# A routed feed-forward kernel: token rows scattered as two planes of 16-bit halves, transposed by the DMA that loads them

## The chip, the cores and the metric

One core of a Trainium2 chip runs the whole program. The metric is device time in microseconds from launch to end, the median of three runs. Every time below is in microseconds (us) unless it says nanoseconds (ns).

## The reference

4096 tokens of 128 features go through three blocks, all in float32: half a feed-forward block with experts, an attention block, and the expert block once more.

```python
x = x + 0.5 * ffn(layernorm(x))
x = x + attn(layernorm(x))
x = x + 0.5 * ffn(layernorm(x))

def ffn(x):
    t = rmsnorm(x) * norm_scale
    vals, idx = top_k(t @ gate_w.T + gate_b, 4)      # 4 of 32 experts
    w = softmax(vals)
    combine[token, idx] = w
    h = swiglu(einsum('th,efh->tef', t, w1) + b1)     # 128 -> 2*128
    out = einsum('tef,ehf->th', h * combine, w2) + combine @ b2
    return x + out
```

Only the four chosen experts of a token count, so the kernel computes those alone. The attention block is linear in the tokens (no softmax over scores) and is not touched by the change.

## The kernel before, in words

**Two chunks, four phases.** The tokens are 32 tiles of 128, in two chunks of 16 tiles (c = 0, 1). An expert block is run twice (f = 0, 1), so there are four phases, ph = 2f + c. In `route` each phase normalises its tiles into `U`, turns them on TensorE, computes the gate, takes the top four, and works out for each of the 64 pairs (tile, choice) the row of a table in device memory to which each token goes.

**Scatter, experts, gather.** GpSimd (`scatter`, L519) issues 64 indirect DMAs a phase. Each writes 128 token rows of 512 bytes from `U` to the table `xs[c]`, sorted by expert, each expert's part padded to a multiple of 128 rows. The table has 96 tiles of 128 rows. `experts` takes it in groups of four tiles (GT = 4), 24 groups a chunk (NG), 48 a block (NGF). SyncE loads a group as 256 KB into `xrow` (L356) and stores its result `yrow` to `ys[c]` (L361). GpSimd (`gather`, L544) then fetches the rows back with 64 indirect DMAs a phase, and VectorE adds them with their weights to `X`.

**The step of the experts.** It is a software pipeline over the groups. In step k TensorE turns the four tiles of `xrow` of group k (`turn_rows`) and those of `hid` of group k-3 (`turn_hid`), forms the first product of group k-1 (four matrix products with 256 columns, `first_product`, L1311) and the second product of group k-4 (`second_product`, L1320). ScalarE copies the second product of group k-5 to `yrow` (L626), computes the gated function of group k-2 (L631), copies the turned `hid` of group k-3 to `hidT` (L634) and the turned rows of group k to `xT`, adding 1.0 (L639). VectorE clips the two halves of the first product (L1005, L1010) and multiplies them (L1018), and in some steps adds a gathered tile to `X` (L981). `xrow`, `xT`, `hid`, `hidT` and `yrow` have two buffers each. In PSUM the turned rows have two banks, the two first products two each, the turned `hid` one (`HT`) and the second product one (`YP`).

**The seam.** Group 24 is the first of chunk 1, and its rows are there only when all 64 DMAs of scatter(1) have landed. `seam` on TensorE and ScalarE writes out by hand the order around it: the work left over of chunk 0 stands interleaved with the start of chunk 1.

**What orders GpSimd.** Its order is fixed: scatter 0, scatter 1, gather 0, gather 1, scatter 2, scatter 3, gather 2, gather 3. Single DMAs also wait for the progress of the experts (`keep_to_experts`, L464: DMA i of a phase waits for a semaphore of a group number worked out from 36·i and an offset). A gather starts only when all 24 groups of its chunk are stored. Scatter 0 runs before the experts of block 0 start, scatter 1 and gather 0 beside them, gather 1 and scatter 2 beside attention and routing, scatter 3 and gather 2 beside the experts of block 1, and gather 3 alone at the end.

## Time and profile before

| | before |
|---|---|
| median of 3 runs | 724.93 us (724.14 to 725.18) |
| span of the profiled execution | 722.9 us |
| mean granted TensorE clock | 0.843 |
| TensorE busy | 531.0 us, 73% |
| weight loads | 443.8 us, 61% |
| VectorE busy | 436.2 us, 60% |
| ScalarE busy | 347.2 us, 48% |
| GpSimd busy | 506.2 us, 70% |
| moved by DMA | 108.28 MB, 150 GB/s over the span |

The median of the runs lies 2.0 us above the span of the profiled execution; the page gives the span, from the first instruction to the last. A busy share is an average over the whole program. The experts of block 0 lie at about 115 to 290 us, those of block 1 at about 460 to 633 us, attention and routing between them, and the last gather after them. GpSimd's 70% leave out about 0.3 us between two indirect DMAs, in which it is neither waiting for anybody nor free.

### The profile page before, as it was taken

How to read it: one execution, taken by the hardware profiler on the slowest of the kernel's cores; microseconds unless marked ns; L12 is line 12 of the kernel's file. 1: busy time of each engine (PE TensorE's matmuls, PEld its weight loads, DVE VectorE, ACT ScalarE, POOL GpSimd, SP SyncE). 2: the span in 40 equal slices, each digit the busy share in tenths (PEclk: the TensorE clock that was granted, in tenths of full speed). 3: DMA queues.
4: the chain of work that ended last, by engine and by line, in shares of the span. 5: the costliest groups of instructions: out<-in, count | busy, mean ns of one | idle time of the engine just before them, and what ended most of it. 6: DMA issues, size and time to landing. Idle time of an engine off the chain costs nothing. (4 is left out here: it accounts for less than half of the span.)

```text
span 722.9 us, 12843 instructions
## 1 busy us (share of the span) xinstructions
PE 531.0 (73%) x3252; PEld 443.8 (61%) x3253; DVE 436.2 (60%) x1243; ACT 347.2 (48%) x752; POOL 506.2 (70%) x551
## 2 busy tenths in 40 slices
PE   6258879999899999385607854999999999933000
PEld 3154366999899998253504553699998999833000
DVE  6889233555547778378993868255564767845222
ACT  4444413666556666495606644366665666610000
POOL 3677777777527777777677777777752777767765
PEclk9556999999999999797557955999999999977555
DMA  7997115566546664222111111456655666524222
GB/s 271 392 375 289 52 54 153 197 194 200 175 147 197 199 210 154 81 54 53 48 52 54 51 52 55 138 182 208 203 168 177 201 198 206 160 78 128 66 62 58
DMA packets 56493, 108.28 MB, mean 150 GB/s; under 512 B 12576, under 2 KB 19968, under 8 KB 56320
## 3 DMA queue, kind: packets, MB, share of 16 engines
q1 hardware_dynamic: 40064, 74.13, 30.7%
q0 software_dynamic: 16384, 33.59, 16.1%
q8 instruction: 23, 0.38, 0.2%
q14 instruction: 22, 0.18, 0.1%
...
## 5 line engine op out<-in xcount | busy, mean ns | idle before, releaser
L564 POOL DMA_INDIRECT YG<-ys,row x256 | 245.0, 957 | 116.9 <-issue 75.4
L539 POOL DMA_INDIRECT xs<-U,row x256 | 250.7, 979 | 81.9 <-issue 74.6
L1311 PE MATMUL PS<-W,xT 128*128 x768 | 182.2, 380 | 0.2
L1311 PEld LDWEIGHTS PS<-W,xT 128*128 128x128 f32 x768 | 138.4, 190 | 16.1 <-issue 1.2
L1005 DVE TENSOR_SCALAR glulin<-PS 128x512 f32<-128x512 f32 x96 | 66.3, 691 | 127.8 <-PE PS L1320 84.3
L626 ACT ACTIVATE yrow<-PS 128x512 f32<-128x512 f32 x96 | 57.3, 597 | 103.3 <-PE PS L1320 103.3
L1320 PEld LDWEIGHTS PS<-W,hidT 128*128 128x128 f32 x768 | 100.7, 193 | 7.8 <-issue 3.4
L1320 PE MATMUL PS<-W,hidT 128*128 x768 | 102.8, 277 | 1.6 <-issue 1.2
L1018 DVE SCALAR_TENSOR_TENSOR hid<-glulin,swish 128x512 f32<-128x512 f32 x96 | 66.6, 694 | 16.0 <-ACT swish L631 10.5
L631 ACT ACTIVATE swish<-glulin 128x512 f32<-128x512 f32 x96 | 60.4, 629 | 30.5 <-DVE glulin L1005 26.7
L639 ACT ACTIVATE xT<-PS 128x512 f32<-128x512 f32 x96 | 56.3, 589 | 38.8 <-PE PS L1214 38.7
L1010 DVE TENSOR_SCALAR glulin<-PS 128x512 f32<-128x512 f32 x96 | 65.3, 680 | 0.0
L1214 PE MATMUL PS<-ident,xrow 128*128 128x128 f32 x384 | 58.5, 275 | 3.9 <-DMA xrow<-xs 3.8
L1214 PE MATMUL PS<-ident,hid 128*128 128x128 f32 x384 | 58.1, 274 | 1.9 <-ACT hidT L634 1.9
L634 ACT ACTIVATE hidT<-PS 128x512 f32<-128x512 f32 x96 | 55.6, 579 | 0.9 <-PE PS L1214 0.9
L1214 PEld LDWEIGHTS PS<-ident,xrow 128*128 128x128 f32 x384 | 45.4, 142 | 7.3 <-DMA xrow<-xs 6.5
L1214 PEld LDWEIGHTS PS<-ident,hid 128*128 128x128 f32 x384 | 45.2, 141 | 2.3 <-DVE hid L1018 2.3
L1063 DVE SCALAR_TENSOR_TENSOR PS<-YG,wtop,X 128x128 f32<-128x128 f32 x40 | 12.4, 353 | 50.5 <-issue 44.5
L981 DVE SCALAR_TENSOR_TENSOR X<-YG,wtop,X (+1 forms) x96 | 32.8, 341 | 3.9 <-DMA YG<-ys,row 3.9
L1214 PE MATMUL PS<-ident,U 128*128 128x128 f32 x64 | 14.5, 386 | 24.7 <-ACT U L595 24.7
L1231 PEld LDWEIGHTS PS<-gw,xT 128*128 128x128 f32 x128 | 25.8, 296 | 6.0 <-issue 3.6
L583 ACT ACTIVATE vq<-vq 128x32 f32<-128x32 f32 x6 | 1.4, 229 | 58.2 <-DVE vq L808 58.2
...
## 6 DMA issues: line engine op xcount, KB each, us to landing
xrow<-xs SPq DMA_DIRECT2D x96, 256.0 KB
ys<-yrow SPq DMA_DIRECT2D x96, 256.0 KB
...
xs<-U,row POOLq DMA_INDIRECT x256
YG<-ys,row POOLq DMA_INDIRECT x256, 2.5
out<-X SPq DMA_DIRECT2D x7, 256.0 KB, 2.6
X<-in_x SPq DMA_DIRECT2D x4, 256.0 KB, 3.6
```

Source lines behind the costliest of these rows:

```text
L539: pool.indirect_dma_start(out=xs[c], out_offset=bass.IndirectOffsetOnAxis(ap=row[:, i:i + 1], axis=0), in_=U[:, (c * CT + t) * H:(c * CT + ...
L564: pool.indirect_dma_start(out=YG[:, t * TOPK + k, :], out_offset=None, in_=ys[c], in_offset=bass.IndirectOffsetOnAxis(ap=row[:, i:i + 1], ...
L626: a.activation(yrow[:, r, :], bank, ACT.Copy).then_inc(yrow_ready, 1)
L631: a.activation(swish[:, r, :], glu[:, r, :], ACT.Gelu_apprx_sigmoid).then_inc(swish_ready, 1)
L634: a.activation(hidT[:, r, :], HT, ACT.Copy).then_inc(hidT_ready, 1)
L639: a.activation(xT[:, r, :], TP[r], ACT.Copy, bias=1.0).then_inc(xT_ready, 1)
L1005: v.tensor_scalar(glu[:, s, :].rearrange("p (q f) -> p q f", q=GT), h1[:, 0], LIMIT, None, ALU.min).then_inc(glu_ready, 1)
L1010: v.tensor_scalar(lin[:, s, :].rearrange("p (q f) -> p q f", q=GT), h1[:, 1], -LIMIT, LIMIT, ALU.max, ALU.min).then_inc(lin_ready, 1)
L1018: v.scalar_tensor_tensor(hid[:, s, :], lin[:, s, :], 1.0, swish[:, s, :], ALU.add, ALU.mult)\
L1214: last = te.transpose(dst[:, q * P:(q + 1) * P], src[:, q * H:(q + 1) * H], ident[:])
L1311: last = te.matmul(h1, xT[:, r, q * P:(q + 1) * P], W[:, bass.ds(es[q], 2 * H)], start=True, stop=True)
L1320: last = te.matmul(bank[:, q * H:(q + 1) * H], hidT[:, r, q * P:(q + 1) * P], W[:, bass.ds(es[q] + 2 * H, H)], start=True, stop=True)
```

## The change

The normalised rows are no longer scattered as float32. In `route`, after the copies to `xT`, ScalarE adds 1.0 to four tiles of `U` at a time (into `hid`, which is free there) and then copies them to `planes`, where a token has 128 low halves of 16 bits and behind them 128 high halves, 512 bytes as before. These rows are scattered. The DMA that loads a group is a transposing DMA over 16-bit elements: it reads 512 rows of 256 halves and writes `xP` with 128 partitions of two planes of 512 halves. TensorE no longer turns rows; ScalarE's `join_rows` puts low and high halves together into `xT` (1024 elements of 16 bits a partition). The two PSUM banks that become free go to the turned `hid` and the second product, so that both have two. `U` shrinks to one chunk, and a few buffers are laid over others to make room for `planes`.

The seam is written in another order on TensorE, ScalarE and SyncE: chunk 0 is finished before chunk 1 starts. The offset of the gathers in `keep_to_experts` goes from 2750 to 2380.

```diff
-        U = sb("U", [P, NTILE * H])
+        U = sb("U", [P, CT * H])
+        planes = sb("planes", [P, NTILE * 2 * H], U16)
-        xrow = sb("xrow", [P, 2, GW])
+        xP = sb("xP", [P, 2, 2 * GW], U16)
-        HT = PS[:, 6, :]
-        YP = PS[:, 7, :]
+        HT = [PS[:, 0, :], PS[:, 6, :]]
+        YP = [PS[:, 7, :], PS[:, 1, :]]
-        xs_v = [a.rearrange("(g p q) h -> g p (q h)", p=P, q=GT) for a in xs]
+        xs_v = [a.bitcast(U16).rearrange("(g r) n -> g r n", r=GW) for a in xs]
...
                 def load(c, k, r):
-                    wait_count(sp, turned, k + (t0 - 4 if c == 0 and isinstance(k, int) and k < 2 else t0 - 1))
-                    sp.dma_start(xrow[:, r, :], xs_v[c][bass.ds(k, 1)].rearrange("g p n -> (g p) n"))\
+                    wait_count(sp, xT_ready, k + (f * NGF + c * NG - 1))
+                    sp.dma_start_transpose(xP[:, r, :].rearrange("p (w n) -> p w n", w=2),
+                                           xs_v[c][bass.ds(k, 1)].rearrange("g r n -> (g r) n"))\
                         .then_inc(xrow_loaded[r], 16)
...
-                held = {1: (NG - 5, NG - 4), 2: (NG - 3,), 3: (NG - 2,), 4: (NG - 1,)}
+                held = {1: (NG - 2, NG - 1)}
                 for c in range(NCHUNK):
                     if c:
-                        store(c - 1, NG - STORE_LAG, (NG - STORE_LAG) % 2)
+                        for n in range(NG - STORE_LAG, NG - 2):
+                            store(c - 1, n, n % 2)
                     sp.wait_ge(scattered[c], 16 * PAIRS * (f + 1))
...
-                k, part = divmod((36 * i + (2750 if c else -100)) // 10, 10)
+                k, part = divmod((36 * i + (2380 if c else -100)) // 10, 10)
...
                         pool.indirect_dma_start(
-                            out=xs[c], out_offset=bass.IndirectOffsetOnAxis(ap=row[:, i:i + 1], axis=0),
-                            in_=U[:, (c * CT + t) * H:(c * CT + t + 1) * H], in_offset=None,
+                            out=xs[c].bitcast(U16), out_offset=bass.IndirectOffsetOnAxis(ap=row[:, i:i + 1], axis=0),
+                            in_=planes[:, (c * CT + t) * 2 * H:(c * CT + t + 1) * 2 * H], in_offset=None,
                         ).then_inc(scattered[c], 16)
...
+                for q in range(NRG):
+                    Q, i = ph * NRG + q, (c * CT + q * GT) * 2 * H
+
+                    act.wait_ge(u_done, CT // 2 * ph + (q + 1) * (GT // 2))
+                    act.wait_ge(u2_done, CT // 2 * ph + (q + 1) * (GT // 2))
+                    wait_count(act, planes_ready, Q - 1)
+                    a.activation(hid[:, q % 2, :], U[:, q * GW:(q + 1) * GW], ACT.Copy, bias=1.0).then_inc(lifted, 1)
+                    act.wait_ge(lifted, Q + 1)
+                    a.activation(planes[:, i:i + 2 * GW].rearrange("p (t w h) -> p t w h", w=2, h=H),
+                                 hid[:, q % 2, :].bitcast(U16).rearrange("p (t h w) -> p t w h", w=2, h=H), ACT.Copy)\
+                        .then_inc(planes_ready, 1)
...
-                def copy_rows(n, r):
-                    act.wait_ge(turned, n + (t0 + 1))
+                def join_rows(n, r, m):
+                    act.wait_ge(xrow_loaded[r], (m + (g0 // 2 + 1)) * 16)
                     wait_count(act, multiplied, n + (m0 - 1))
-                    a.activation(xT[:, r, :], TP[r], ACT.Copy, bias=1.0).then_inc(xT_ready, 1)
+                    a.activation(xT[:, r, :].bitcast(U16).rearrange("p (q n w) -> p q n w", q=GT, w=2),
+                                 xP[:, r, :].rearrange("p (w n q) -> p q n w", q=GT, w=2), ACT.Copy).then_inc(xT_ready, 1)
...
-                def turn_rows(n, r, m):
-                    pe.wait_ge(xrow_loaded[r], (m + (g0 // 2 + 1)) * 16)
-                    wait_count(pe, xT_ready, n + (g0 - 1))
-                    return turn(TP[r], xrow[:, r, :], GT)
...
                 def seam():
                     k = NG
-                    turn_hid(k - 3, 1).then_inc(seam_turned, 1)
+                    turn_hid(k - 3, 1)
                     first_product(k - 1, 1).then_inc(multiplied, 1)
-                    second_product(k - 4, 0, YP, k - 4).then_inc(seam_multiplied, 1)
-                    turn_rows(k, 0, k // 2).then_inc(turned, 1)
-                    second_product(k - 3, 1, YP, k - 3).then_inc(seam_multiplied, 1)
-                    turn_hid(k - 2, 0).then_inc(seam_turned, 1)
-                    turn_rows(k + 1, 1, k // 2).then_inc(turned, 1)
-                    second_product(k - 2, 0, YP, k - 2).then_inc(seam_multiplied, 1)
-                    turn_hid(k - 1, 1).then_inc(seam_turned, 1)
+                    second_product(k - 4, 0).then_inc(seam_multiplied, 1)
+                    turn_hid(k - 2, 0)
+                    second_product(k - 3, 1).then_inc(seam_multiplied, 1)
+                    turn_hid(k - 1, 1)
+                    second_product(k - 2, 0).then_inc(seam_multiplied, 1)
+                    second_product(k - 1, 1).then_inc(seam_multiplied, 1)
                     first_product(k, 0).then_inc(multiplied, 1)
-                    second_product(k - 1, 1, YP, k - 1).then_inc(seam_multiplied, 1)
-                    turn_rows(k + 2, 0, k // 2 + 1).then_inc(turned, 1)
                     first_product(k + 1, 1).then_inc(multiplied, 1)
```

**One step of the experts on TensorE**, inside the loop, up to the first matrix product. PS is PSUM, `eid` the list of the groups' experts. Before:

```order
L1214 MATMUL PS<-ident,xrow 128x128 x4
L1214 MATMUL PS<-ident,hid 128x128 x4
L1289 ISA
L1289 TENSOR_LOAD eid
L1306 REGISTER_ALU
L1311 ISA
L1311 MATMUL PS<-W,xT 128x256
```

After:

```order
L1230 MATMUL PS<-ident,hid 128x128 x4
L1304 ISA
L1304 TENSOR_LOAD eid
L1316 REGISTER_ALU
L1321 ISA
L1321 MATMUL PS<-W,xT 128x256
```

The four turns of the loaded rows are gone and nothing stands in their place.

**SyncE at the seam**, behind the loop of chunk 0: `ys<-yrow` is a store, the other one a load. Before:

```order
L361 DMA ys<-yrow 128x512
L356 DMA xrow<-xs 128x512 x2
L361 DMA ys<-yrow 128x512 x2
L356 DMA xrow<-xs 128x512
L361 DMA ys<-yrow 128x512
```

After:

```order
L364 DMA ys<-yrow 128x512 x4
L358 DMA_TRANSPOSE xP<-xs 128x2x512 x2
L364 DMA ys<-yrow 128x512 x2
L358 DMA_TRANSPOSE xP<-xs 128x2x512 x5
L364 DMA ys<-yrow 128x512
```

The first load of chunk 1 is the instruction that waits for scatter 1. Four stores of chunk 0 stand ahead of it now, one did before; the last two of chunk 0 stand right behind the first two loads of chunk 1, where before the last one stood behind the fifth.

**ScalarE at the seam**, from the first instruction behind the loop of chunk 0. Before:

```order
L626 ACTIVATE yrow<-PS 128x512
L631 ACTIVATE swish<-glulin 128x512
L634 ACTIVATE hidT<-PS 128x512
L626 ACTIVATE yrow<-PS 128x512
L631 ACTIVATE swish<-glulin 128x512
L626 ACTIVATE yrow<-PS 128x512
L634 ACTIVATE hidT<-PS 128x512
L639 ACTIVATE xT<-PS 128x512 x2
L626 ACTIVATE yrow<-PS 128x512
L634 ACTIVATE hidT<-PS 128x512
L626 ACTIVATE yrow<-PS 128x512
```

After:

```order
L645 ACTIVATE yrow<-PS 128x512
L650 ACTIVATE swish<-glulin 128x512
L654 ACTIVATE hidT<-PS 128x512
L645 ACTIVATE yrow<-PS 128x512
L650 ACTIVATE swish<-glulin 128x512
L654 ACTIVATE hidT<-PS 128x512
L645 ACTIVATE yrow<-PS 128x512
L654 ACTIVATE hidT<-PS 128x512
L645 ACTIVATE yrow<-PS 128x512 x2
L659 ACTIVATE xT<-xP 128x1024 x2
```

The first two `xT` of chunk 1 stood ahead of the last two `yrow` of chunk 0; now they stand behind all of them, and each has 1024 elements of 16 bits where it had 512 of 32.

## Rows read from the trace of the kernel before

**Rows 1.** Page, part 4: the chain that ended last, by engine.

```profile
POOL 8%; issue 4%; DMA 1%; PE 0%; DVE 0%; ACT 0%; POOLq 0%; ACTq 0%
```

**Rows 2.** Timeline of GpSimd: start, duration, engine, line, instruction, count, [idle before <-releaser].

```profile
210.94 0.97 POOL L564 DMA_INDIRECT YG<-ys,row  x1 [17.62 <-ACT hidT L634]
293.47 0.94 POOL L564 DMA_INDIRECT YG<-ys,row  x1 [1.02 <-issue]
...
537.12 1.04 POOL L539 DMA_INDIRECT xs<-U,row  x1 [0.30 <-ACT hidT L634]
554.38 0.97 POOL L564 DMA_INDIRECT YG<-ys,row  x1 [16.22 <-DMA ys<-yrow]
...
636.69 0.94 POOL L564 DMA_INDIRECT YG<-ys,row  x1 [1.57 <-issue]
```

**Rows 3.** Windows, ten steps of chunk 0: length, busy per engine, clock, DMA share, GB/s.

```profile
153.92:188.85 34.93, 34.93 (x242) 32.87 (x241) 19.81 (x30) 21.98 (x40) 27.00 (x27) 1.00 0.63 199
```

**Rows 4.** Timeline of TensorE: one step, and the same place ten steps on.

```profile
153.92 0.60 PE L1214 MATMUL PS<-ident,xrow 128*128 128x128 f32 x4
154.36 0.60 PE L1214 MATMUL PS<-ident,hid 128*128 128x128 f32 x4
...
188.85 0.60 PE L1214 MATMUL PS<-ident,xrow 128*128 128x128 f32 x4
```

**Rows 5.** Timeline of TensorE: groups 0, 23, 24 and the end, both blocks.

```profile
115.52 1.99 PE L1311 MATMUL PS<-W,xT 128*128 x8
...
192.78 1.89 PE L1311 MATMUL PS<-W,xT 128*128 x8
...
197.36 0.65 PE L1214 MATMUL PS<-ident,xrow 128*128 128x128 f32 x4 [1.79 <-DMA xrow<-xs]
...
203.25 1.89 PE L1311 MATMUL PS<-W,xT 128*128 x8
...
288.82 1.15 PE L1320 MATMUL PS<-W,hidT 128*128 x8 [0.22 <-issue]
...
546.72 1.89 PE L1311 MATMUL PS<-W,xT 128*128 x8
...
631.65 1.15 PE L1320 MATMUL PS<-W,hidT 128*128 x8 [0.22 <-issue]
```

**Rows 6.** Timeline of SyncE at the seams: start, time of issue, instruction, count.

```profile
194.61 0.82 SPq L356 DMA_DIRECT2D xrow<-xs  x2
...
539.45 0.82 SPq L356 DMA_DIRECT2D xrow<-xs  x2
```

**Rows 7.** Groups by line and shape, ScalarE: count, busy, mean ns, idle before.

```profile
L631 ACT ACTIVATE swish<-glulin 128x512 f32<-128x512 f32 x96 | 60.4, 629 | 30.5 <-DVE glulin L1005 26.7 <-issue 0.4
L626 ACT ACTIVATE yrow<-PS 128x512 f32<-128x512 f32 x96 | 57.3, 597 | 103.3 <-PE PS L1320 103.3
L634 ACT ACTIVATE hidT<-PS 128x512 f32<-128x512 f32 x96 | 55.6, 579 | 0.9 <-PE PS L1214 0.9
...
L766 ACT ACTIVATE glulin<-PS 128x1024 f32<-128x1024 f32 x4 | 3.9, 1021 | 14.3 <-PE PS L1214 14.3
```

**Rows 8.** DMA, 150 to 180 us: packets, MB, share of 16 engines; issues and size.

```profile
q1 hardware_dynamic: 2423, 4.41, 48.5%
q0 software_dynamic: 736, 1.51, 14.8%
...
ys<-yrow SPq DMA_DIRECT2D x9, 256.0 KB
xrow<-xs SPq DMA_DIRECT2D x8, 256.0 KB
xs<-U,row POOLq DMA_INDIRECT x23
```

**Rows 9.** Windows, a stretch of the first seam, columns as in rows 3.

```profile
200.00:202.00 2.00, 2.00 (x10) 1.68 (x9) 0.00 (x0) 1.74 (x4) 0.00 (x0) 0.50 0.50 190
```

**Rows 10.** Timeline of ScalarE, first instruction of the second phase's routing.

```profile
42.60 0.23 ACT L583 ACTIVATE vq<-vq 128x32 f32<-128x32 f32 x1 [15.53 <-DVE vq L808]
```

138 lines of the change are left out of this document (68 added, 70 removed).

## Prediction

> **What bounds the kernel now.** I read the chain of waits first, then GpSimd's timeline from end to end, then the two stretches of experts. The chain that ended last shows GpSimd alone with some issue time [rows 1]: the last gather. GpSimd's timeline explains the rest. From its first scatter on, its indirect DMAs follow each other at about 1.29 us (64 gathers and one wait of 1.0 between 210.94 and 293.47 [rows 2]), and only two waits are long: 17.6 us ahead of gather 0 and 16.2 us ahead of gather 2, both at a seam [rows 2]. GpSimd is the clock of the program, and a change pays only by what it takes from these two waits, and by not letting gathers 1 and 3 start later than GpSimd is ready for them.
>
> What those waits hang on is the pace of the experts. Ten steps of chunk 0 take 34.93 us, TensorE is busy for all of it, at full granted clock [rows 3]: 3.49 us a step, bound by TensorE. At the seam the load of group 24 goes out when scatter 1 has landed, at 194.61 [rows 6]; its rows are turned from 197.36, but its first product starts only at 203.25, since work of chunk 0 stands between, and the last second product ends at 288.82 + 1.15 = 289.97 [rows 5]. Gather 1 starts at 293.47 with a wait of only 1.0 [rows 2]. So the experts and gather 0 end together there, and both must come earlier for a gain. Block 1 is alike: load at 539.45 [rows 6], first product of group 24 at 546.72, end at 631.65 + 1.15 = 632.80 [rows 5], gather 3 at 636.69 after a wait of 1.6 [rows 2].
>
> **The change part by part.**
>
> *Turns removed.* The four turns of a group take 154.36 - 153.92 = 0.44 us of TensorE's time [rows 4]. The step becomes 3.05 us, if TensorE stays the bound.
>
> *ScalarE's join.* It replaces a copy of 512 elements by one of 1024. The nearest row is L766 with 1024 elements of 32 bits, 1.02 us; its other three instructions a step are 0.63 + 0.60 + 0.58 = 1.81 [rows 7]. Together 2.83, under 3.05. ScalarE's order lets the join of group k+1 end about 2.9 us after the end of TensorE's step k, and the product that needs it starts at 3.05 + 0.44 = 3.49, so 0.6 us is spare. Bounds for the unseen copy (16-bit elements, planes 1024 bytes apart): 0.6, the 512-element copy, and 2.0, twice L766. I take 1.04, by element count. At 2.0 ScalarE would need 3.8 us a step and be the bound.
>
> *Transposed load.* The window of 30 us has 17 transfers of 256 KB on the hardware queue, in 48.5% of the DMA engines' time: 14.55 / 17 = 0.86 us each; 23 scatters take 14.8%, 0.19 us each [rows 8]. In a step of 3.05 us a store (0.86) and 2.4 scatters (0.46) leave 1.73 us for the load. No row shows a transposing DMA. Lower end: the plain load's 0.86, as it moves the same bytes. Upper end: the load breaks into 512 x 2 pieces of one plane row (256 bytes), and each costs what a packet costs now, 14.55 x 16 / 2423 = 0.096 us [rows 8]: 64 pieces an engine, 6.1 us. I take 1.0, near the plain row, because the source is contiguous and the bytes are the same; the other end stays as a rival. In time to landing the loads have 5.0 us from issue (join k-2 done) to use (join k); the plain one at the seam took 197.36 - 194.61 = 2.75 [rows 5, 6]. Behind a late load ScalarE waits in the join, and behind that stand its copies of y and hid, so TensorE waits too. On SyncE the next store stands behind each load; it has over 4 us to spare.
>
> The Trainium skill, page DMA: Bandwidth & Descriptors, section Latency and other measured facts, gives a transposing DMA 261 GB/s where the pieces are not contiguous; 256 KB would take 1.0 us by that, an estimate, and the sum would not change. The same skill's page VectorE: DVE Perf Modes, section The three transpose paths, speaks against the change: 1309 ns for a 128 x 128 block by DMA against 390 ns by TensorE. No run so far shows either; for the second see the fourth rival.
>
> *First seam.* From the first product of group 0 to that of group 23 it took 192.78 - 115.52 = 77.3 us [rows 5]. Without 22 turns that is 9.7 less: 183.1. From there to the last second product of the chunk: chunk 1 needed 289.97 - 203.25 = 86.7 for the same way plus its drain, so the drain is 9.4. Chunk 0 ends at 192.5, its last copy at 193.1, before scatter 1 has landed at 194.6. So scatter 1 decides from here: load out at 194.6, rows at 197.4, join 1.04, first product of group 24 at 198.5, 4.8 earlier than before. Against it stands TensorE's idle time from 192.5 to 198.5. Before, it idled 1.8 us ahead of 197.36 [rows 5], and the clock granted at 200 to 202 was 0.50, the lower of its two levels [rows 9]. I take 2.0 us lost for a stretch of 4 us at half speed, within 0 and 4. Then chunk 1: 86.7 - 23 x 0.44 = 76.6. End 277.1, and 3.5 us as before for copy and store (293.47 - 289.97): gather 1 may start at 280.6.
>
> Gather 0 waits for the stores of groups 22 and 23, which stand behind two loads that wait for scatter 1: 194.61 + 0.8 of issue, more if a transposing load holds SyncE longer, + 2.9 to landing. I take 199.5. Its 64 DMAs need 82.5 - 1.0 = 81.5: it ends at 281.0. The later one decides: gather 1 at 281.0 instead of 293.47, **12.5 us gained**. The waits that the code puts into gather 0 advance 0.36 group per DMA, 1.1 us of experts, and don't bind.
>
> *Second seam.* Load 539.45, first product of group 24 at 543.3 + 2.0 lost; chunk 1 took 632.80 - 546.72 = 86.1, now 76.0; end 621.3, + 3.5: 624.8. Gather 2 starts at 544.4 (539.45 + the same 4.9) and needs 636.69 - 554.38 - 1.3 = 81.0: 625.4 instead of 636.69, **11.3 us gained**.
>
> *Planes.* Eight instructions a phase on ScalarE, 4 x (0.6 + 1.02) = 6.5 us [rows 7]. In phase 0 they fall into 15.5 us of idle time before 42.60 [rows 10], and the first plane is ready well before the first scatter; in phases 2 and 3 the scatter has to wait for the gather or scatter ahead of it on GpSimd anyway. Cost 0; without cover at most 6.5 a phase. Scattered bytes and row counts are unchanged, so I leave GpSimd's 0.96 us a DMA; bounds 0 and, for twice the element count, some 0.1.
>
> *Two banks for hid and y.* They take waits away that TensorE's full busy time shows to be covered. 0.
>
> *Sum.* 722.9 - 12.5 - 11.3 = 699.1 us of span, + 2.0 between span and median = 701.1. I add 1.4 for steps of VectorE that also add a gathered tile, where the spare 0.6 us shrinks: **702.5 us**. Its own range, by 0 to 4 for the clock, 0 to 1 for landing and 0 to 0.1 us a step: 698 to 708.
>
> **The rivals.** What the step's length is worth: up to 3.2 us only chunk 1 counts, 23 us per us of step and block. Above it chunk 0 ends after scatter 1, and both chunks count, 46 a block. The gain is gone at a step of 3.40: from 280.6 + 23 x 0.18 the rest to 293.5 is used up at 3.42 in block 0, at 3.37 in block 1. Beyond that it costs 92 us per us.
>
> 1. *Partly.* The step settles at 3.25, for a join of 1.6 us or loads that land after 5 us now and then. 702.5 + 46 x 0.2 = 712 us. For it: 0.6 us of slack is little, and all engines meet in it. Against: DMA engines are busy only 63% [rows 3].
> 2. *The other side: the transposed load is dear.* Place: DMA engines in both stretches of experts. Price: midway between the bounds, 3.3 us a load; the step is then 3.3 + 0.86 + 0.46 = 4.6 and the time 725 + 92 x 1.2 = 835 us. It decides from 2.1 us a load on (3.40 - 1.32), 2.4 times the plain one. For it: the unseen upper end lies at 7 times. Against: same bytes, contiguous rows.
> 3. *ScalarE becomes the bound.* A join of 1.8 us or more: 1.81 + 1.8 = 3.6, 725 + 92 x 0.2 = 743 us. Against: durations of ScalarE go by element count in every row.
> 4. *Each piece costs a packet.* The upper bound above, 6.1 us a load: DMA then sets a step of 6.1 + 1.32 = 7.4 and the time is 725 + 92 x 4.0 = 1093 us. For it: nothing in the rows excludes it. Against: packets now carry 1.8 KB (4.41 MB in 2423 [rows 8]), so a piece of 256 bytes should take less. By the Trainium skill's 1309 ns a block (VectorE: DVE Perf Modes, The three transpose paths) eight blocks one after another would be 10.5 us a load, an estimate, and worse still.
> 5. *It doesn't do what it says.* Steps get shorter, but gather 0 still starts where it did, held by a wait for the experts or by the two late stores. 724 us. For it: before, such a wait ended the idle time of 17.6 us [rows 2].
>
> **How the numbers follow.** Forecast 0.50, rival 1 0.18, rival 2 0.20, rival 3 0.05, rival 4 0.04, rival 5 0.03. Faster by over 0.2% (1.4 us, about what a measurement tells from no change): 0.69, with a hundredth of the others. Within: 0.03. Slower: 0.28. For the range of 8 in 10: from 697 it must take in the forecast, rivals 1, 3 and 5 and the near edge of rival 2, which reaches down to 725: 697 to 745. The likeliest case alone has 698 to 708.
>
> **What would show it.** In the profile after: TensorE's steps 3.05 us apart in chunk 0, with no waits; joins of 1.0 us; GpSimd's waits at the seams 6 us instead of 17.6 and 16.2; gather 1 from 281 and gather 3 some 24 us earlier than before; a clock of 0.5 for some us after each seam. It is wrong if ScalarE idles ahead of the join for a DMA, if the DMA share in the experts' stretch is near 1, or if the seam's waits stay and TensorE has gaps in each step.

## The result, and the profile after

| | before | after |
|---|---|---|
| median of 4 runs each, same chip | 724.85 us (724.14 to 725.18) | 713.52 us (712.26 to 716.13) |
| ratio, 95% interval | | 0.9866 (0.9851 to 0.988) |
| span of the profiled execution | 722.9 us | 710.5 us |
| ScalarE busy | 347.2 us, 48% | 455.6 us, 64% |
| TensorE busy | 531.0 us, 73% | 504.9 us, 71% |
| GpSimd busy | 506.2 us, 70% | 507.7 us, 71% |

The change gains 11.3 us. The forecast was a gain of 22.4 us, to 702.5 us; the time lies in its range of 697 to 745, but outside the 698 to 708 of its likeliest case and next to rival 1, "partly", with 712 us.

The chain that ended last is still GpSimd's, as in [rows 1]:

```profile
POOL 8%; issue 4%; DMA 1%; ACT 0%; DVE 0%; POOLq 0%; ACTq 0%
```

GpSimd's timeline, with the last scatters, the first gathers at the two seams and gathers 1 and 3, answers to [rows 2]:

```profile
189.85 0.96 POOL L545 DMA_INDIRECT xs<-planes,row  x1 [0.30 <-issue]
200.28 0.97 POOL L570 DMA_INDIRECT YG<-ys,row  x1 [9.47 <-issue]
285.36 1.06 POOL L570 DMA_INDIRECT YG<-ys,row  x1 [2.96 <-issue]
...
530.24 0.96 POOL L545 DMA_INDIRECT xs<-planes,row  x1 [0.30 <-issue]
541.53 0.97 POOL L570 DMA_INDIRECT YG<-ys,row  x1 [10.33 <-issue]
624.74 0.94 POOL L570 DMA_INDIRECT YG<-ys,row  x1 [0.89 <-issue]
```

The waits at the seams fell from 17.62 and 16.22 us to 9.47 and 10.33, not to about 6. By their starts, gather 0 came 10.7 us earlier (210.94 - 200.28; forecast 11.4) and gather 2 12.85 us (554.38 - 541.53). Gather 1 starts 8.1 us earlier than before (293.47 - 285.36; forecast 12.5) and gather 3 11.95 us earlier (636.69 - 624.74; forecast 23.8).

The main reason stands in ScalarE's groups, which answer to [rows 7] (count, busy us, mean ns, idle before):

```profile
L659 ACT ACTIVATE xT<-xP 128x1024 uint16<-128x1024 uint16 x96 | 144.8, 1512 | 36.3 <-DMA xP<-xs 36.2
L650 ACT ACTIVATE swish<-glulin 128x512 f32<-128x512 f32 x96 | 60.4, 629 | 23.1 <-DVE glulin L1019 17.9
L654 ACT ACTIVATE hidT<-PS 128x512 f32<-128x512 f32 x96 | 55.7, 580 | 1.0 <-PE PS L1230 1.0
```

The join takes 1.51 us. Its 36.2 us of idle time for the load are seven waits; 17.56 us of them lie ahead of the first join of block 0 and 14.8 at the start of block 1. Beyond the first steps of a block and the seams only two are left, of 1.1 and 0.5 us, so in a usual step the join doesn't wait for its load. The copies into `planes` (L624), the same 1024 elements of 16 bits, take 1.06. Fourteen steps of chunk 0, columns as in [rows 3]:

```profile
142.43:187.17 44.74, 44.71 (x282) 40.24 (x281) 27.73 (x42) 42.84 (x57) 34.22 (x35) 1.00 0.79 215
```

A step is 44.74 / 14 = 3.20 us, 0.15 more than forecast. ScalarE, the fourth number of busy time, is busy for 42.84 of the 44.74 us; before it was 21.98 of 34.93. TensorE is shown as busy for 44.71 us too, so this row alone doesn't tell which of the two sets the step; the experiments do. ScalarE's timeline in one step has one gap, 0.22 us:

```profile
142.63 0.60 ACT L645 ACTIVATE yrow<-PS 128x512 f32<-128x512 f32 x1
143.45 0.63 ACT L650 ACTIVATE swish<-glulin 128x512 f32<-128x512 f32 x1 [0.22 <-DVE glulin L1019]
143.99 0.58 ACT L654 ACTIVATE hidT<-PS 128x512 f32<-128x512 f32 x1
144.46 1.51 ACT L659 ACTIVATE xT<-xP 128x1024 uint16<-128x1024 uint16 x1
145.88 0.58 ACT L645 ACTIVATE yrow<-PS 128x512 f32<-128x512 f32 x1
```

In chunk 1, where VectorE also adds gathered tiles, 18 steps take 269.75 - 210.94 = 58.8 us, 3.27 each. The two rows are starts of first products on TensorE's timeline. No idle time is marked there, but the starts show where a step is longer than 3.05: from 140 to 186 us it took on average 0.50 us from the turn to the first product (0.44 before), and 1.80 us from there to the second product (1.73 before).

```profile
210.94 1.25 PE L1321 MATMUL PS<-W,xT 128*128 x5
...
269.75 1.56 PE L1321 MATMUL PS<-W,xT 128*128 x6
```

The DMA queues from 150 to 180 us, as in [rows 8]:

```profile
q1 hardware_dynamic: 11437, 4.88, 64.8%
q0 software_dynamic: 768, 1.57, 15.4%
...
ys<-yrow SPq DMA_DIRECT2D x10, 256.0 KB
xs<-planes,row POOLq DMA_INDIRECT x24
xP<-xs SPq DMA_TRANSPOSE x10
```

The hardware queue took 0.648 x 30 = 19.44 us for ten stores at 0.86 and ten loads: (19.44 - 8.6) / 10 = 1.08 us a transposing load. The packets went from 2423 to 11437. At 143 for a store as before (2423 / 17), some 1000 are left for a load, as the forecast's upper end supposed; but a piece costs 1.08 x 16 / 1024 = 0.017 us of one DMA engine, and not the 0.096 that a packet cost before.

256 KB in 1.08 us are 242 GB/s. The Trainium skill (DMA: Bandwidth & Descriptors, Latency and other measured facts) gives 261 GB/s, by which a load would take 1.0 us, an estimate; the trace agrees within 8%. The Trainium skill's 1309 ns for one 128 x 128 block (VectorE: DVE Perf Modes, The three transpose paths), from which the prediction estimated 10.5 us for eight blocks one after another, is not what a block costs here: 1.08 / 8 = 0.14 us.

TensorE at the first seam (group 24 from 198.76), then the seam's loads on SyncE and the joins on ScalarE, answer to [rows 5, 6]:

```profile
194.27 1.15 PE L1330 MATMUL PS<-W,hidT 128*128 x8 [0.19 <-issue]
198.76 3.52 PE L1321 MATMUL PS<-W,xT 128*128 x8 [3.34 <-ACT xT L659]
```

```profile
193.55 2.58 SPq L358 DMA_TRANSPOSE xP<-xs  x2
196.18 1.05 SPq L364 DMA_DIRECT2D ys<-yrow  x2
```

```profile
194.23 0.60 ACT L645 ACTIVATE yrow<-PS 128x512 f32<-128x512 f32 x1 [0.61 <-DMA ys<-yrow]
195.46 0.60 ACT L645 ACTIVATE yrow<-PS 128x512 f32<-128x512 f32 x1 [0.64 <-PE PS L1330]
197.13 2.91 ACT L659 ACTIVATE xT<-xP 128x1024 uint16<-128x1024 uint16 x2 [1.07 <-DMA xP<-xs]
```

Chunk 0's last second product ends at 195.4 instead of 192.5. The load of group 24 leaves at 193.55: the stores of chunk 0 ahead of it, which wait for ScalarE's copies, are out at 192.87, and scatter 1, which left GpSimd at 190.81 (189.85 + 0.96), had the last word by 0.6 us. At the second seam the stores alone hold it. Scatter 3 left GpSimd at 531.20 (530.24 + 0.96), the stores went out until 534.75, and the load followed at once:

```profile
SPq L358 <- DMA xs<-planes,row: 0.6, 1, 0.6
...
524.35 10.40 SPq L364 DMA_DIRECT2D ys<-yrow  x5
534.85 2.63 SPq L358 DMA_TRANSPOSE xP<-xs  x2
```

The first row is a wait of SyncE at the first seam: waiting line, what for, us in total, times, longest. Two transposing loads hold SyncE for 2.58 us, where two plain ones held it for 0.82 [rows 6]; only then come the two stores on which gather 0 waits. From issue to its join the first load took 197.13 - 193.55 = 3.6 us, 0.8 more than the plain one. TensorE idles 3.34 us, and its clock is at the lower of its two levels behind that, as in [rows 9]:

```profile
200.00:202.00 2.00, 2.00 (x6) 1.55 (x6) 0.00 (x0) 0.03 (x1) 1.42 (x2) 0.53 0.95 184
202.00:204.00 2.00, 2.00 (x10) 1.43 (x8) 1.49 (x3) 0.86 (x2) 1.46 (x2) 1.00 0.65 146
```

### The profile page after: what moved, and what is told of

It reads as the page before. It is cut to its first block and busy times, and to the rows that moved or that the text cites. A ratio compares the mean times of both kernels' runs of the same rounds, so it can differ in the third digit from the quotient of the medians.

```text
span 710.5 us, 11944 instructions
## 1 busy us (share of the span) xinstructions
PE 504.9 (71%) x2868; PEld 408.8 (58%) x2869; DVE 436.0 (61%) x1243; ACT 455.6 (64%) x784; POOL 507.7 (71%) x551
## 2 busy tenths in 40 slices
DMA packets 144043, 108.25 MB, mean 152 GB/s; under 512 B 112416, under 2 KB 119808, under 8 KB 143872
## 5 line engine op out<-in xcount | busy, mean ns | idle before, releaser
L545 POOL DMA_INDIRECT xs<-planes,row x256 | 249.9, 976 | 81.4 <-issue 71.3
L1321 PE MATMUL PS<-W,xT 128*128 x768 | 192.2, 395 | 17.8 <-ACT xT L659 16.4
L1321 PEld LDWEIGHTS PS<-W,xT 128*128 128x128 f32 x768 | 141.8, 194 | 46.5 <-issue 28.5
L659 ACT ACTIVATE xT<-xP 128x1024 uint16<-128x1024 uint16 x96 | 144.8, 1512 | 36.3 <-DMA xP<-xs 36.2
L1391 PE MATMUL PS<-qkvW,hidT 128*128 128x384 f32 x64 | 29.1, 539 | 0.0
L1246 PE MATMUL PS<-gw,xT 128*128 128x32 f32 x128 | 25.9, 362 | 3.9 <-DVE topi L859 3.0
```

What stands on the lines that cost most here:

```text
L545: pool.indirect_dma_start(out=xs[c].bitcast(U16), out_offset=bass.IndirectOffsetOnAxis(ap=row[:, i:i + 1], axis=0), in_=planes[:, (c * CT ...
L659: a.activation(xT[:, r, :].bitcast(U16).rearrange("p (q n w) -> p q n w", q=GT, w=2), xP[:, r, :].rearrange("p (w n q) -> p q n w", q=GT, ...
L1321: last = te.matmul(h1, xT[:, r, q * P:(q + 1) * P], W[:, bass.ds(es[q], 2 * H)], start=True, stop=True)
```

## The experiments

The first theory: ScalarE's join is the bound of a step, by the way it walks through memory. The rivals: the transposing DMA, the order at the seam, VectorE. Each ratio is against the kernel before on the same chip. Except for the first four, that kernel took 723.1 to 724.1 us there, and the change, which ran on another chip, has 0.9866 on that scale. "Under the change" means 713.5 less the median of the run; the ratios give sizes that differ from these by less than 1 us.

### First look: four kernels on another chip

On this chip the kernel before took 855.91 us (853.12 to 857.92), with waits of some 2 us strewn over all engines. So only durations of single instructions are taken from it, no times.

Half join:

```diff
-                    a.activation(xT[:, r, :].bitcast(U16).rearrange("p (q n w) -> p q n w", q=GT, w=2),
-                                 xP[:, r, :].rearrange("p (w n q) -> p q n w", q=GT, w=2), ACT.Copy).then_inc(xT_ready, 1)
+                    a.activation(xT[:, r, :].bitcast(U16).rearrange("p (q n w) -> p q n w", q=GT, w=2)[:, :, :, 1],
+                                 xP[:, r, :].rearrange("p (w n q) -> p q n w", q=GT, w=2)[:, :, :, 1], ACT.Copy).then_inc(xT_ready, 1)
```

> Leaves out the copy of the low halves in the join: ScalarE's join handles the 512 high halves only, so xT keeps old low halves. Everything else is the changed kernel. Theory A (ScalarE's join of 1.51 us sets the step of 3.20 us): the join falls to 0.8 us or less, ScalarE has slack again, TensorE's step falls to 3.05 us, chunk 0 ends about 3 us earlier, gather 1 and gather 3 each start 3 to 4 us earlier, 704 to 707 us. Theory B (the transposed load or the DMA engines, busy 80 to 98% of these stretches, set the step): the step stays near 3.2 and the time at 713.

Measured: join 0.77 us; 870.07 us, ratio 1.0151 (1.0086 to 1.0216).

Plain load:

```diff
-        xs_v = [a.bitcast(U16).rearrange("(g r) n -> g r n", r=GW) for a in xs]
+        xs_v = [a.bitcast(U16).rearrange("(g p q) n -> g p (q n)", p=P, q=GT) for a in xs]
...
-                    sp.dma_start_transpose(xP[:, r, :].rearrange("p (w n) -> p w n", w=2),
-                                           xs_v[c][bass.ds(k, 1)].rearrange("g r n -> (g r) n"))\
+                    sp.dma_start(xP[:, r, :], xs_v[c][bass.ds(k, 1)].rearrange("g p n -> (g p) n"))\
                         .then_inc(xrow_loaded[r], 16)
...
-                                 xP[:, r, :].rearrange("p (w n q) -> p q n w", q=GT, w=2), ACT.Copy).then_inc(xT_ready, 1)
+                                 xP[:, r, :].rearrange("p (q w n) -> p q n w", q=GT, w=2), ACT.Copy).then_inc(xT_ready, 1)
```

> The load is a plain DMA of the same 256 KB instead of a transposing one, so the rows reach TensorE untransposed; the join puts the halves together as before, but the two planes of a row now lie 256 bytes apart. Theory A: the join still takes about 1.5 us if any jump between two planes costs the same, the step stays 3.2, and only the shorter hold of SyncE (0.34 instead of 1.23 us a load) is gained at the seams: 711 to 713 us. Theory B: with the transposition gone DMA is busy as before the change, the step falls to 3.05 and the time to 705 or less.

Measured: join 1.16 us, SyncE held 0.34 us a load; 865.29 us, ratio 1.0103 (1.0066 to 1.014).

Old order at the seam (TensorE, ScalarE, SyncE), with planes; TensorE's part:

```diff
                     first_product(k - 1, 1).then_inc(multiplied, 1)
                     second_product(k - 4, 0).then_inc(seam_multiplied, 1)
+                    second_product(k - 3, 1).then_inc(seam_multiplied, 1)
                     turn_hid(k - 2, 0)
-                    second_product(k - 3, 1).then_inc(seam_multiplied, 1)
+                    second_product(k - 2, 0).then_inc(seam_multiplied, 1)
                     turn_hid(k - 1, 1)
-                    second_product(k - 2, 0).then_inc(seam_multiplied, 1)
+                    first_product(k, 0).then_inc(multiplied, 1)
                     second_product(k - 1, 1).then_inc(seam_multiplied, 1)
-                    first_product(k, 0).then_inc(multiplied, 1)
```

> The seam's order on TensorE, ScalarE and SyncE is put back to the one before the change; planes, transposed load, join and the double banks stay. Theory A with the seam as the second part of the gain: the last copies and stores of chunk 0 stand again behind the joins and loads of chunk 1, gather 0 and gather 2 start 6 to 10 us later, and the time is 720 to 726 us, so that without the new seam the shorter step brings almost nothing. Rival (the shorter step brings the gain by itself, the seam's order does not matter): 713 us.

Measured: join 1.51 us; 887.59 us, ratio 1.0364 (1.0326 to 1.0402).

Join with the two planes outside:

```diff
-                    a.activation(xT[:, r, :].bitcast(U16).rearrange("p (q n w) -> p q n w", q=GT, w=2),
-                                 xP[:, r, :].rearrange("p (w n q) -> p q n w", q=GT, w=2), ACT.Copy).then_inc(xT_ready, 1)
+                    a.activation(xT[:, r, :].bitcast(U16).rearrange("p (q n w) -> p w q n", q=GT, w=2),
+                                 xP[:, r, :].rearrange("p (w n q) -> p w q n", q=GT, w=2), ACT.Copy).then_inc(xT_ready, 1)
```

> The same join with the same operands, but the order in which it goes through the elements is plane, tile, token instead of tile, token, plane: reads step 8 bytes and writes 4 bytes, and it does not jump 1024 bytes between planes at each element. Theory A1 (the jump between the planes makes the join 1.51 us where the planes copy with the same 1024 elements takes 1.06): the join takes 1.05 to 1.1 us, the step falls to 3.05 to 3.1, 704 to 707 us. Theory A2 (16-bit elements written with a stride, or the DMA writing xP beside it, make it long): the join stays at 1.4 to 1.5 us and the time at 713.

Measured: join 1.35 us; 873.21 us, ratio 1.0209 (1.0175 to 1.0243). The four durations say that the cost of the join hangs on its access pattern, not on the number of elements alone. The times are left out of the argument.

### Join that reads in order

```diff
-                    a.activation(xT[:, r, :].bitcast(U16).rearrange("p (q n w) -> p q n w", q=GT, w=2),
-                                 xP[:, r, :].rearrange("p (w n q) -> p q n w", q=GT, w=2), ACT.Copy).then_inc(xT_ready, 1)
+                    a.activation(xT[:, r, :].bitcast(U16).rearrange("p (q n w) -> p w n q", q=GT, w=2),
+                                 xP[:, r, :].rearrange("p (w n q) -> p w n q", q=GT, w=2), ACT.Copy).then_inc(xT_ready, 1)
```

> The changed kernel with the join going through the elements in the order plane, token, tile: it reads 1024 halves that lie one behind the other and writes with steps of 512 bytes. Joins seen so far: 1.51 us where reads jump 1024 bytes between planes, 1.35 us where they step 8 bytes, 1.16 us where planes lie 256 bytes apart. Theory A1 (the read pattern makes the join long): 1.02 to 1.1 us as in the planes copy, the step falls to 3.05, 704 to 707 us on a chip where the kernel before takes 725. Theory A2 (any 16-bit join of a transposed load is long, or the writes pay instead): 1.35 us or more, 709 to 713 us.

Measured: 977.95 us (975.38 to 979.18), ratio 1.352 (1.3478 to 1.3563). Its join by the trace (min, median and max ns):

```profile
L659 ACT ACTIVATE xT<-xP x96: 4711/4747/5012, 113.6 to 872.5; 128x1024 uint16<-128x1024 uint16 x96
```

The reads run on now and the writes jump 512 bytes each, and the copy takes three times as long. So it isn't jumps in the reads alone that cost; theory A2, by which the writes pay, had the direction, but not the size. In this kernel ScalarE is busy for 45.00 us of 45 (142 to 187 us) and TensorE for 30.03, so ScalarE does set the pace when its join is that long.

### Half join, on a usual chip

```diff
-                    a.activation(xT[:, r, :].bitcast(U16).rearrange("p (q n w) -> p q n w", q=GT, w=2),
-                                 xP[:, r, :].rearrange("p (w n q) -> p q n w", q=GT, w=2), ACT.Copy).then_inc(xT_ready, 1)
+                    a.activation(xT[:, r, :].bitcast(U16).rearrange("p (q n w) -> p q n w", q=GT, w=2)[:, :, :, 1],
+                                 xP[:, r, :].rearrange("p (w n q) -> p q n w", q=GT, w=2)[:, :, :, 1], ACT.Copy).then_inc(xT_ready, 1)
```

> Leaves out the copy of the low halves in the join, as the earlier run of the same kernel, whose chip ran the kernel before at 856 us, with single waits of 2 us and more that the other executions don't have. Theory A (ScalarE's join sets the step): with a join of 0.77 us the step is 3.05 us and the ratio to the kernel before 0.970 to 0.975 (703 to 707 us of 725). Theory B (transposed load or DMA engines set it): step 3.2, ratio 0.985.

Measured: 707.52 us (706.28 to 708.66), ratio 0.9775 (0.9743 to 0.9807), 6.0 us under the change. Join 0.77 us; steps of chunk 0 of 3.10 us (17 in 52.74), those of chunk 1 of 3.16. So the join's length costs the change about 6 us, a little less than theory A expected. Gather 1 starts 2.0 us earlier than in the change (283.38 for 285.36) and gather 3 4.4 us (620.34 for 624.74). Here too TensorE idles ahead of group 24, 5.81 us.

### Old seam, on a usual chip

The edit of the old order above; this is SyncE's part of it. `keep_to_experts` keeps the offset of 2380, and the turned `hid` and the second product their two banks each.

```diff
-                held = {1: (NG - 2, NG - 1)}
+                held = {1: (NG - 5, NG - 4), 2: (NG - 3,), 3: (NG - 2,), 4: (NG - 1,)}
...
-                        for n in range(NG - STORE_LAG, NG - 2):
-                            store(c - 1, n, n % 2)
+                        store(c - 1, NG - STORE_LAG, (NG - STORE_LAG) % 2)
```

> The old order of the seam on TensorE, ScalarE and SyncE with planes, transposed load and double banks, run again. Theory A: gather 0 and gather 2 start 6 to 10 us later than in the changed kernel, 720 to 726 us. Rival (the shorter step brings the gain whatever the seam's order): 713 us.

Measured: 734.98 us (731.44 to 737.62), ratio 1.0169 (1.0125 to 1.0214): slower than before by 11 to 12 us, and than the change by 21.5. GpSimd's two waits at the seams:

```profile
211.27 0.97 POOL L569 DMA_INDIRECT YG<-ys,row  x1 [21.43 <-DMA ys<-yrow]
...
562.17 0.97 POOL L569 DMA_INDIRECT YG<-ys,row  x1 [21.82 <-issue]
```

Gather 0 starts at 211.27 (210.94 before), although chunk 0's steps are as short as in the change. In this order the last store of chunk 0 stands behind the fifth load of chunk 1, and leaves at 208.13. ScalarE's joins, which wait for the loads of chunk 1, stand ahead of its last copies for chunk 0, and TensorE idles 5.11 us for one of these. Planes with the old order are slower than the kernel before.

### Warm seam

```diff
+                    pe.wait_ge(glu_ready, k + (g0 - 1))
+                    pe.wait_ge(lin_ready, k + (g0 - 1))
+                    for i in range(10):
+                        te.matmul(H1[0][:, 0:GW], ones[:], ones[:, 0:1].broadcast_to([P, GW]), start=True, stop=True)
                     first_product(k, 0).then_inc(multiplied, 1)
```

> The changed kernel with ten products of ones (0.27 us each at full clock) in TensorE's queue between chunk 0's last product and the first one of chunk 1, in the gap in which it waits for the join. If the granted clock of 0.53 to 0.62 at 198 to 202 us comes from that gap and costs 2.0 us a seam: first products of groups 24 and 25 at full speed, gather 1 up to 2 us earlier, gather 3 at most 0.6 us more (GpSimd decides there), 711 us. Rival (the clock there costs nothing that isn't hidden): 713.5 us.

Measured: 710.15 us (708.91 to 710.85), ratio 0.9808 (0.9779 to 0.9838), 3.4 us under the change. The window behind the idle time:

```profile
200.00:202.00 2.00, 2.00 (x10) 1.42 (x8) 1.50 (x3) 0.63 (x1) 1.69 (x2) 1.00 0.97 159
```

The clock stays at its upper level, 1.00 in place of 0.53. The first two first products of chunk 1 take 3.72 us here and 5.25 in the change, at the second seam 3.71 and 5.39: 1.5 and 1.7 us a seam, where the forecast had 2.0. That agrees with the 3.4 us between the medians, though the two profiled executions differ by 1.4 us only.

### Stores ahead of the second load

```diff
-                held = {1: (NG - 2, NG - 1)}
+                held = {0: (NG - 2, NG - 1)}
```

> At the seam SyncE issues the stores of groups 22 and 23 behind the first transposing load, ahead of the second. Theory (the two loads hold SyncE 2.6 us ahead of the stores that gather 0 waits for, and chunk 0's late drain does the rest): the stores leave 1.2 us earlier, gathers 0 and 2 start 1 us earlier, first product of group 24 stays (its own load is the first), the load of group 25 leaves 1 us later with room to spare. Time 711.5 to 713 against 713.5 of the change. Rival (gathers 0 and 2 are held by the copies and stores of the last groups, wherever SyncE stands): no difference, 713.5. Second rival (the end of chunk 1, not of gather 0, decides gather 1): gather 0 earlier, its longer way full of waits, 713.5 too.

Measured: 714.54 us (712.06 to 715.74), ratio 0.9866 (0.9849 to 0.9882): no difference. Gather 0 starts at 200.13 (200.28 in the change). By SyncE's timeline the two stores begin at 195.50, 0.7 us earlier, but there was an idle time between load and stores: they waited for ScalarE's copies. So moving the loads away doesn't help this kernel: the copies of chunk 0's last groups are not ready sooner.

### Planes outside and warm seam

Nothing of the computation is left out.

```diff
-                    a.activation(xT[:, r, :].bitcast(U16).rearrange("p (q n w) -> p q n w", q=GT, w=2),
-                                 xP[:, r, :].rearrange("p (w n q) -> p q n w", q=GT, w=2), ACT.Copy).then_inc(xT_ready, 1)
+                    a.activation(xT[:, r, :].bitcast(U16).rearrange("p (q n w) -> p w q n", q=GT, w=2),
+                                 xP[:, r, :].rearrange("p (w n q) -> p w q n", q=GT, w=2), ACT.Copy).then_inc(xT_ready, 1)
...
+                    pe.wait_ge(glu_ready, k + (g0 - 1))
+                    pe.wait_ge(lin_ready, k + (g0 - 1))
+                    for i in range(10):
+                        te.matmul(H1[0][:, 0:GW], ones[:], ones[:, 0:1].broadcast_to([P, GW]), start=True, stop=True)
```

> The join goes plane by plane on the outside (order plane, token, column) and ten products of ones keep TensorE busy ahead of the first product of chunk 1; the computation is whole. Theory (ScalarE's join of 1.51 us makes ScalarE the bound of a step, the rest of the loss is the clock at the seam): join 1.35 us, step 3.05 to 3.10 instead of 3.20, TensorE busy for all of it, time 704 to 707. Rival (the join's length is not what bounds the step; the join is waited for with its load): step stays 3.2 and the time is that of the warm seam alone, 710.

Measured: **707.32 us** (706.79 to 709.24), ratio 0.9776 (0.9762 to 0.979), 6.2 us under the change, and faster than both kernels beyond the intervals. Join 1.35 us, steps of 3.13 us in chunk 0 and 3.26 in chunk 1. The warm seam alone has 710.15 us, so the shorter join adds about 2.8; the ratios' intervals of the two just overlap.

### The same with the stores ahead of the second load

```diff
-                held = {1: (NG - 2, NG - 1)}
+                held = {0: (NG - 2, NG - 1)}
```

> The edits of e7 and e9 together. Theory: with chunk 0 no longer late, the stores behind the loads are what gathers 0 and 2 wait for, so their order is worth 1 us each seam where gather 0's end decides: 703 to 706, up to 2 us under e9. Rival: chunk 1's end decides, no difference to e9.

Measured: 708.36 us (706.05 to 712.15), ratio 0.9791 (0.9769 to 0.9814), no difference to the last. Gather 0 did start 1.0 us earlier (199.00 for 200.01) and gather 1 1.8 us (282.55 for 284.38), but gather 3 came only 0.4 us earlier (620.93 for 621.33), after a wait of 3.32 us for the end of the experts.

### The new order alone

The kernel before, its turns on TensorE, its plain loads and its single banks for the turned `hid` and the second product kept (SyncE, GpSimd and TensorE; ScalarE's order and a wait on VectorE go with it):

```diff
-                held = {1: (NG - 5, NG - 4), 2: (NG - 3,), 3: (NG - 2,), 4: (NG - 1,)}
+                held = {1: (NG - 2, NG - 1)}
...
-                        store(c - 1, NG - STORE_LAG, (NG - STORE_LAG) % 2)
+                        for n in range(NG - STORE_LAG, NG - 2):
+                            store(c - 1, n, n % 2)
...
-                k, part = divmod((36 * i + (2750 if c else -100)) // 10, 10)
+                k, part = divmod((36 * i + (2380 if c else -100)) // 10, 10)
...
+                    turn_hid(k - 2, 0).then_inc(seam_turned, 1)
+                    second_product(k - 3, 1, YP, k - 3).then_inc(seam_multiplied, 1)
+                    turn_hid(k - 1, 1).then_inc(seam_turned, 1)
+                    second_product(k - 2, 0, YP, k - 2).then_inc(seam_multiplied, 1)
+                    second_product(k - 1, 1, YP, k - 1).then_inc(seam_multiplied, 1)
                     turn_rows(k, 0, k // 2).then_inc(turned, 1)
-                    second_product(k - 3, 1, YP, k - 3).then_inc(seam_multiplied, 1)
-                    turn_hid(k - 2, 0).then_inc(seam_turned, 1)
                     turn_rows(k + 1, 1, k // 2).then_inc(turned, 1)
-                    second_product(k - 2, 0, YP, k - 2).then_inc(seam_multiplied, 1)
-                    turn_hid(k - 1, 1).then_inc(seam_turned, 1)
                     first_product(k, 0).then_inc(multiplied, 1)
-                    second_product(k - 1, 1, YP, k - 1).then_inc(seam_multiplied, 1)
```

> The kernel before with the new order at the seam alone (last second products, then the turns of the next chunk; the two late stores behind two loads; gather 0's waits set for an earlier start). No planes, plain loads, TensorE turns the rows. Theory (order and pace both are needed: gather 0 starts some 4 us earlier, near 207 instead of 210.9, but the experts of chunk 1 end no earlier, since their 23 steps still take 3.49 us each): gather 1 unchanged within 1 us, gather 0 full of waits, 722 to 725. Rival (the order at the seam brings the gain by itself): 713 to 717. Second rival (the order alone costs, as TensorE stands idle ahead of chunk 1 without shorter steps to pay for it): 727 to 732.

Measured: 730.27 us (727.49 to 731.63), ratio 1.0083 (1.0066 to 1.01), 6 us slower than before. GpSimd:

```profile
204.49 0.97 POOL L565 DMA_INDIRECT YG<-ys,row  x1 [11.94 <-issue]
295.48 0.94 POOL L565 DMA_INDIRECT YG<-ys,row  x1 [9.57 <-issue]
...
553.46 0.97 POOL L565 DMA_INDIRECT YG<-ys,row  x1 [11.07 <-issue]
643.21 0.94 POOL L565 DMA_INDIRECT YG<-ys,row  x1 [8.46 <-issue]
```

Gather 0 starts 6.4 us earlier than before, more than expected, and all of it comes back as a wait of 9.57 us ahead of gather 1, since chunk 1 now ends 2.1 us later (292.07 for 289.97). The second rival of this run was right. So planes without the new order lose 11 us, the new order without planes loses 6, and the whole change gains 11.

### Four kernels on what was still missing

At 707 to 708 us, 5 to 6 were still missing to the forecast. Half join with warm seam and stores ahead of the second load. The diffs of these four are against the kernel with all three edits:

```diff
-                    a.activation(xT[:, r, :].bitcast(U16).rearrange("p (q n w) -> p w q n", q=GT, w=2),
-                                 xP[:, r, :].rearrange("p (w n q) -> p w q n", q=GT, w=2), ACT.Copy).then_inc(xT_ready, 1)
+                    a.activation(xT[:, r, :].bitcast(U16).rearrange("p (q n w) -> p q n w", q=GT, w=2)[:, :, :, 1],
+                                 xP[:, r, :].rearrange("p (w n q) -> p q n w", q=GT, w=2)[:, :, :, 1], ACT.Copy).then_inc(xT_ready, 1)
```

> The three edits of e10 with a join that copies only the high halves (512 elements; the low halves of the gathered rows are left out of the product). Theory 1 (ScalarE is what still keeps the step of chunk 1 long): steps of 3.05 us in chunk 1 too, 700 to 703 us. Theory 2 (VectorE, which adds gathered tiles there, or DMA does): steps stay at 3.15 to 3.4, 704 to 707.

Measured: 704.17 us (702.66 to 705.29), ratio 0.9739 (0.9722 to 0.9756). GpSimd's first gathers at the seams:

```profile
197.99 0.97 POOL L570 DMA_INDIRECT YG<-ys,row  x1 [7.05 <-issue]
...
533.60 0.97 POOL L570 DMA_INDIRECT YG<-ys,row  x1 [7.13 <-issue]
```

The waits are 7.1 us, near the 6 of the forecast, and none above 0.8 us is left ahead of gathers 1 and 3. Steps of chunk 1: 3.15 us, which fits theory 2 of the expectation and not theory 1. Of the 0.1 us over 3.05, half lies between the starts of the first and the second product (1.78 us; 1.73 before) and 0.04 between the turn and the first product (0.47; 0.44 before).

Adds of gathered tiles on 8 of 128 columns:

```diff
+                    xt = xt[:, 0:8]
-                    v.scalar_tensor_tensor(xt, YG[:, bass.ds(t * TOPK + j, 1), :]...
+                    v.scalar_tensor_tensor(xt, YG[:, bass.ds(t * TOPK + j, 1), 0:8]...
```

> e10 with VectorE's add of a gathered tile during the experts on 8 of 128 columns (the other columns of these sums are left out), the count of instructions and all waits as they were. Theory 1 (ScalarE): no difference to e10, 708. Theory 2 (VectorE's adds of 0.34 us, 2.4 a step, close the ring from TensorE's product over VectorE and ScalarE back): an add takes some 0.1 us less, steps of chunk 1 fall from 3.25 towards 3.1, 704 to 706. Theory 3 (DMA): no difference.

Measured: 707.66 us (706.15 to 712.12), ratio 0.9795 (0.9754 to 0.9837): no difference. An add took 0.22 us instead of 0.34, and the steps of chunk 1 3.16 us instead of 3.22, yet gather 1 started at 282.39 (282.55 without the edit), since gather 0 had started 1.1 us later there.

Both:

```diff
+                    a.activation(xT[:, r, :].bitcast(U16).rearrange("p (q n w) -> p q n w", q=GT, w=2)[:, :, :, 1],
+                                 xP[:, r, :].rearrange("p (w n q) -> p q n w", q=GT, w=2)[:, :, :, 1], ACT.Copy).then_inc(xT_ready, 1)
...
+                    xt = xt[:, 0:8]
```

> Both edits, e13 and e14. Theories 1 and 2 together: TensorE bound in both chunks, steps of 3.05, 700 to 702 us, which is what was forecast. Theory 3 (the transposing loads with the stores and gathers fill the DMA engines to 0.9 and more in chunk 1): steps stay above 3.15, 704 or more.

Measured: 705.22 us (703.05 to 706.03), ratio 0.9744 (0.9719 to 0.9769). Steps of chunk 1 took 3.13 us, against 3.15 with the half join alone. VectorE's adds are at most a small part of what is missing.

Plain load with warm seam and stores ahead:

```diff
-        xs_v = [a.bitcast(U16).rearrange("(g r) n -> g r n", r=GW) for a in xs]
+        xs_v = [a.bitcast(U16).rearrange("(g p q) n -> g p (q n)", p=P, q=GT) for a in xs]
...
-                    sp.dma_start_transpose(xP[:, r, :].rearrange("p (w n) -> p w n", w=2),
-                                           xs_v[c][bass.ds(k, 1)].rearrange("g r n -> (g r) n"))\
+                    sp.dma_start(xP[:, r, :], xs_v[c][bass.ds(k, 1)].rearrange("g p n -> (g p) n"))\
                         .then_inc(xrow_loaded[r], 16)
...
-                                 xP[:, r, :].rearrange("p (w n q) -> p q n w", q=GT, w=2), ACT.Copy).then_inc(xT_ready, 1)
+                                 xP[:, r, :].rearrange("p (q w n) -> p q n w", q=GT, w=2), ACT.Copy).then_inc(xT_ready, 1)
```

> The three edits of e10 with a plain DMA in the place of the transposing one (same bytes, rows not turned, so the product gets them in another order; join of 1.16 us as that read order took before). Theories 1 and 2: the load is not what counts, the gain is that of a join 0.2 us shorter, 704 to 707. Theory 3 (the transposing loads' DMA time and the 1.23 us that each holds SyncE): stores leave sooner, DMA share in chunk 1 falls from 0.94 to some 0.7, gathers 0 and 2 start 2 us earlier, 700 to 703.

Measured: 705.85 us (703.0 to 706.29), ratio 0.9759 (0.9743 to 0.9776). Two windows of 60 us in chunk 1, first the half join with transposing loads, then this kernel (the last but one number is the DMA share):

```profile
210.00:270.00 60.00, 59.80 (x386) 54.77 (x385) 49.16 (x106) 45.02 (x76) 45.83 (x47) 1.00 0.98 212
```

```profile
210.00:270.00 60.00, 59.84 (x386) 54.89 (x385) 49.45 (x107) 52.73 (x77) 45.89 (x47) 1.00 0.70 213
```

DMA engines busy 0.98 or 0.70 of the time, and TensorE does the same 386 products. The joins of the two differ (0.77 and 1.16 us), so a small cost of the busier DMA engines could be hidden behind the longer join; a large one can't. Steps of chunk 0 took 3.10 and 3.08 us. The 2.5 us to the kernel with all three edits are within what a shorter join (1.16 us) gives; the intervals of the two overlap.

## Why the prediction was right or wrong

- **Right: what bounds the program**, GpSimd's waits at the seams, and that a change pays by them alone. Each run's time follows them.
- **Right: the turns.** A step of 3.05 us would be TensorE's; with a short join it came to 3.10 in chunk 0. But that TensorE bounds a step can't be read from its busy time: it is 44.71 us of 44.74 after the change as well, where ScalarE sets the step.
- **Wrong: the term "ScalarE's join", sized 1.04 us "by element count".** It took 1.51. That made ScalarE's sum 1.81 + 1.51 = 3.32 us by durations, 3.20 by pace, since neighbours overlap a little (144.46 + 1.51 = 145.97, the next starts at 145.88). So ScalarE, not TensorE, set the step: 3.20 and 3.27 us. The bounds of 0.6 to 2.0 held it; the value taken was by size when the row it came from (L766) was of 32-bit elements side by side. Taking half of the elements away gave 6.0 us back.
- **Wrong in its wake: "up to 3.2 us only chunk 1 counts".** Chunk 0 ended at 195.4, 2.9 us late. In block 0 that hardly counted, since scatter 1 decided the load even so: gather 0 started at 200.28 for a forecast of 199.5. Gather 1 started 4.4 us late (285.36 for 281.0), 2.96 of it a wait for the end of chunk 1. In block 1 most of the loss was there when chunk 0 ended: with the 8.1 us that block 0 gained added back, the load left 3.5 us late (534.85 + 8.1 for 539.45), gather 2 started 5.2 late (541.53 + 8.1 for 544.4) and gather 3 7.4 late (624.74 + 8.1 for 625.4). I had let the scatter decide both seams; at the second one the stores of chunk 0 did, out at 534.75, where the scatter had left GpSimd at 531.20. So chunk 0 counts below 3.2 already.
- **Near: the clock.** 4.0 us forecast, 2.0 a seam; 3.4 measured by the warm seam, 1.5 and 1.7 a seam by the products themselves.
- **Right: the transposed load's price**, 1.08 us for a forecast of 1.0. Rivals 2 and 4 fell: the load did break into small packets, but each cost a sixth of what the upper end gave it. What I had not priced is SyncE's time, 1.23 us a load instead of 0.4; neither of the two runs that moved the stores past the second load found a time in it.
- **Right: the planes on ScalarE.** The eight instructions a phase, of 1.06 us and less, cost nothing that shows; the first scatter went out at 27.03 (27.91 before).
- **Rival 1** had the mechanism and the size: a join of 1.6 us, a step of 3.25, both chunks counting, 712 us. It had a chance of 0.18 against the forecast's 0.50. Its second reason, loads that land late, gave only the two waits of 1.1 and 0.5 us. **Rival 3**, ScalarE as the bound, is the same mechanism with a longer join; it set in below the 1.8 us that it asked for. A join of 1.16 us went with steps of 3.08 in chunk 0, one of 1.35 with 3.13, one of 1.51 with 3.20. **Rival 5** fell in the change, but is what the old order at the seam does.
- **Slips in the working, none of which moves the forecast by over 0.3 us.** Midway between 0.86 and 6.1 us is 3.5, not 3.3 (rival 2); the time of gather 2's DMAs took off 1.3 us for a wait that the row gives as 1.57; and 1.29 us for one DMA holds the wait of 1.0, without which it is 1.27.
- **The ledger.** 713.5 - 702.5 = 11.0 us were missing. A short join takes 6.0 off, a warm seam 3.4, both with the stores ahead 9.3 (704.2). The warm seam takes off what the forecast had counted as a loss, so against 702.5 - 4.0 = 698.5 some 5.7 us stay open in that kernel. Its steps in chunk 1 are 3.15 us, not 3.05; 0.1 us x 23 steps x 2 blocks are 4.6 us of it. VectorE's adds give 0.02 us of that, and no large cost of the load's DMA time was seen. What holds each step there by 0.1 us wasn't found.
